# Two cross-attention layers with mixtures of experts: zero products at the beginning, undivided GpSimd operations, a new order of work

## The chip, the cores and the metric

One core of a Trainium2 chip runs the kernel. The metric is the device time of one execution in microseconds (us); the median of three runs is 582.1 us (580.37 to 582.15). "fp32" is the usual 32-bit type, "fp32r" a rounded form of it that TensorE multiplies in one pass; an fp32 product of 128x128 by 128 columns is two matmul instructions.

## The reference

The input x has 4 batches of 512 rows of 128 numbers, the context 4 batches of 154 rows. Four layers are added to x, each on the layer norm (ln) of what came before:

```python
x = x + L0_xattn(ln(x), ctx)   # 16 heads of 8 over the 154 context rows, softmax, output product
x = x + L0_ffn(ln(x))          # 8 experts, width 512, gelu, top 2 by a softmax router
x = x + L1_xattn(ln(x), ctx)   # causal self-attention, norm, cross-attention, norm, leaky relu net, norm, relu
x = x + L1_ffn(ln(x))          # 32 experts of width 64 and a shared one, silu(g) * u, 6 of 32 by a sigmoid router
```

Every token is computed by all experts, and the router's weights (zero for those not chosen) multiply the results.

## The kernel before

The batches are the unit of work: stage A (L0_xattn), B (L0_ffn), C (L1_xattn) and D (L1_ffn), each for b = 0 to 3. Stage A runs for all batches first, up to about 135 us. Then B of one batch is interleaved with C of the batch before, and D follows; D of batches 2 and 3 ends the run, alone.

**The order of work** is written out by hand. Each engine's program is a set of generators (stages), each cut into parts by `yield`. `merged` (line 76) reads a table for the engine (PLAN_PE, PLAN_DVE and so on) with a number for each part, and issues the parts in the order of these numbers. The numbers have no other effect: at run time an engine takes its parts in that order, and waits at semaphores. So a new table is a new order of the same steps. SP's table orders the loads (x, context, weights, and the rows of router weights that `spread_first` and `spread_second` write to memory and read back to all partitions), and the store.

**The beginning.** SP issues the loads of x and of the constants (early), ScalarE those of the context, of early_rows and of the mask. ScalarE then runs a small Exp on mhalf (`warm_up`, line 901), with the activation table's load before it. GpSimd clears KN, QN, KS, VT and VM. VectorE normalises x (L425 to L448, with two steps on GpSimd, L454 and L457), and clears WT, gsc and mks (`paddings`, L1189). TensorE's program begins with a wait for the constants. Then follow the products of the context with the key and value weights (L1665), the transposes of the normalised x (L1642), the query product (L1691), the transposes of keys (L1716, L1718) and of QN (L1654), and the first maxima products (L1730), 128x308, whose row maxima VectorE takes (L1302). ScalarE copies the transposes out (L892).

**Stage B.** For each chunk of 128 hidden columns: three products of halves (high and low parts in fp32r, L1647 to L1649), gelu on ScalarE (L1006), and the second product, plain fp32 (L1854) for even chunks and in halves (L1659 to L1661) for odd ones, where ScalarE makes the high half and VectorE the low one (L1359). Four chunks make an expert: VectorE multiplies by the router's row (L1398, ty), and GpSimd adds it to acc_o (L790, called from `stage_b`).

**Stage D.** For each pair of experts (17 with the shared one): six products (L1647 to L1649), silu on ScalarE (L1137), the product with u on VectorE (L1598, one input in PSUM), the product with the router's rows CB (L1604, both inputs in SBUF), and the down product. For batches 0 and 1 that is plain fp32 (L2027). For batches 2 and 3 (`THREE`) ScalarE makes the high half WB_r, GpSimd the low one h_r (`lows_d`, L790), and TensorE does three products (L1659 to L1661), for batch 3 in two halves of the columns.

**GpSimd's operations.** `in_pieces` (L786) cuts a two-input operation into instructions of 256 columns, with one semaphore step after the last. It is used for acc_o (512 columns), the low halves of D (512), the low halves of the weights (`split1`: four of 1024 and one of 256; `split3`: four of 512 and one of 128). `split2` (L823) and norm2b (L878) are cut by loops of their own. The odd down chunk of `shh` has 128 columns.

Of the kernel before, what the change touches and what calls it, by code (L numbers as in the profile page):

```python
# [32 lines left out]
P = 128  # L33
# [58 lines left out]
class Signal:  # L92
# [11 lines left out]
    def then(self):  # L104
# [7 lines left out]
    "constants": [[6, 979, 10456]],  # L112
    "load_x": [[0], [973], [2503], [4860]],
    "load_context": [[856], [4380], [7188]],
    "second_weights": [[16147, 25499, 34539, 35632, 36068, 38842]],
    "load_context1": [[13685], [18833], [30509], [36074]],
    "store": [[43977], [50106], [53327], [56038, 56075]],
    "spread_first": [[13075, 13317, 13323, 14187, 14774, 15464, 16141, 16845, 17432], [18839, 19144, 19150, 19625,
        20571, 21096, 22238, 23076, 23801], [25250, 25493, 25505, 26247, 27091, 27873, 29108, 29590, 30503], [31432,
        31674, 31828, 32987, 33839, 34533, 35626, 36953, 37319]],  # L120
    "spread_second": [[36329, 36929, 36941, 37325, 37337, 39097, 39249, 39412, 40036, 40168, 40629, 40767, 41092,
# [7 lines left out]
    "norm_a": [[570, 598], [1602, 1702], [4147, 4174], [7093, 7121]],  # L129
    "values": [[1620], [4736], [7645], [10442]],  # L130
    "key_tails": [[1803, 1861], [4278, 4560], [7858, 7919], [9331, 11489]],
    "norm_b": [[7726, 7754], [11468, 11547], [16027, 16054], [23214, 23241]],
    "stage_b": [[14690, 14838, 15464, 16158, 16845, 17432, 18020, 18542], [19625, 20571, 21096, 22395, 23076, 24397,
        24544, 24932], [26247, 27091, 27873, 29291, 29590, 30761, 31022, 31828], [34140, 34288, 34533, 35626, 37787,
        37935, 38083, 38417]],
    "split1": [[31631, 35782, 38556, 38832, 41808]],
    "split2": [[12971, 14410]],
    "split3": [[39108, 39972, 40111, 40817, 50723]],
    "lows_d": [[48235, 48748, 48908, 49301, 49440, 49692, 49898, 50038, 50350, 50585, 50939, 51077, 51242, 51569,
        51775, 52038, 52176], [52382, 52709, 52847, 53119, 53325, 53463, 53669, 53875, 54081, 54287, 54493, 54820,  # L140
        54959, 55203, 55341, 55547, 55685]],
    "stage_c": [[18957, 18985, 22264, 22291, 23532, 23559, 24255, 25665, 25692], [25537, 25564, 28559, 28587, 30630,
        30657, 31493, 32807, 32834], [32361, 32388, 35764, 36058, 37150, 37177, 37646, 39277, 39304], [39149, 39176,
        42795, 42822, 44984, 45011, 45723, 47076, 47103]],
    "norm_d": [[29160, 29187], [34120, 34671], [40799, 40955], [48373, 48400]],
}
PLAN_ACT = {
    "warm_up": [[0, 18]],
    "split0": [[2564, 2614, 3385, 3588, 3864, 3913, 4785, 6718]],
    "prepare_a": [[1033], [2663], [5153], [8263]],  # L150
    "query_stacks": [[1512, 1886, 2050, 3257], [3990, 4640, 5334, 5983], [7002, 7697, 7996, 8878], [9548, 10494, 10890,
        11666]],
    "key_stacks": [[1270, 1305, 1340, 1375, 1413, 1561, 1596, 1631], [3135, 3222, 3637, 3777, 4406, 4441, 4476, 4511],
        [6648, 6683, 6819, 6854, 7373, 7460, 7495, 7530], [8994, 9028, 9247, 9281, 10195, 10282, 10317, 10352]],
    "group": [[2110, 2224, 2274, 2339, 2388, 2460], [2712, 2833, 2886, 2996, 3080, 3173, 3435], [3336, 3487, 3539,
# [6 lines left out]
    "output": [[5104], [7938], [10786], [13437]],  # L162
    "prepare_b": [[10992, 12302, 13012], [15446, 18137, 18592], [20899, 22292, 25187], [27171, 29383, 31368]],
# [193 lines left out]
def build_program(nc, a):  # L357
# [1270 lines left out]
    def _(pe):  # L1628
# [4 lines left out]
        def claim(k):  # L1633
            if last_read[k]:
                pe.wait_ge(*last_read[k])
# [497 lines left out]
```

## Time and profile before

| | us |
|---|---|
| median of three runs | 582.1 |
| the profiled execution | 581.68 |
| its span, first to last instruction | 579.9 |
| TensorE busy | 554.4 (96%) |
| VectorE busy | 446.9 (77%) |
| ScalarE busy | 378.5 (65%) |
| GpSimd busy | 190.8 (33%) |

PE is TensorE (PEld its weight loads), DVE VectorE, ACT ScalarE, POOL GpSimd, SP the queue that issues loads. Busy time counts an instruction from start to end; matmuls overlap, so their ends run past the start of the next. In the stages, each engine's busy us is followed by its number of instructions (x...), then come the granted clock of TensorE (1.00 is full), the busy share of the DMA engines and GB/s. A group's row has the line, the engine, the operation, out<-in, the shapes and the count, then busy us and mean ns of one, then idle time before it and what ended it. A row in order of time has start, length, then the same names; equal instructions are merged (x...).

### The profile page before, as it was taken

Reading aid. Unit: us, or ns where it says so; the run is one execution under the profiler, and the core shown is the slowest. Engines: PE = TensorE matmul, PEld = TensorE weight load, DVE = VectorE, ACT = ScalarE, POOL = GpSimd, SP = SyncE. Lnnn points to the kernel's source line nnn. Section 1 sums busy time; section 2 is a strip of 40 time slices with the busy share of each in tenths; the row PEclk is TensorE's granted clock in tenths of the full one; section 3 lists DMA queues with packets and bytes.
Section 4 is the critical chain, followed back from the end, with each engine's and each line's share of the span. In section 5 each row is a group of like instructions: output and inputs, shape, how many; then the busy total and the mean of one; then the engine's idle time right before and its main releaser. Section 6 shows DMA issues by size and latency. Waiting matters only on the chain.

```text
span 579.9 us, 8752 instructions
## 1 busy us (share of the span) xinstructions
PE 554.4 (96%) x2629; PEld 389.6 (67%) x2629; DVE 446.9 (77%) x1343; ACT 378.5 (65%) x663; POOL 190.8 (33%) x265
## 2 busy tenths in 40 slices
PE   4899999999999999999999999999999999999996
PEld 3566566655777677667767677667566766776885
DVE  6898999882454566879577796978988999889774
ACT  2587677757767797757875599865664623565653
POOL 3102020011433112443133413448341011477765
PEclk9999999999999999999999999999999999999998
DMA  4401000301111111003101102441121432432440
GB/s 142 176 20 29 1 9 2 121 25 42 42 47 36 47 37 37 20 18 93 36 20 45 39 19 74 141 110 62 67 90 42 145 92 77 143 114 67 149 151 20
DMA packets 23327, 38.40 MB, mean 66 GB/s; under 512 B 3792, under 2 KB 9552, under 8 KB 22896
## 3 DMA queue, kind: packets, MB, share of 16 engines
q1 hardware_dynamic: 22848, 37.44, 20.6%
q8 instruction: 21, 0.34, 0.2%
q10 hardware_dynamic: 432, 0.40, 0.2%
q14 instruction: 26, 0.21, 0.1%
HBM read 36.45 MB, written 1.38 MB: 65 GB/s over the span
## 4 chain that ended last, share of the span: by engine, by line
PE 72%; DVE 12%; POOL 6%; ACT 4%; issue 4%; DMA 1%; POOLq 0%; DVEq 0%; ACTq 0%
PE ps L1647 9%; PE ps L1649 8%; PE ps L1648 8%; PE ps L1854 7%; PE ps L2027 4%; PE ps L1730 3%; PE ps L1659 3%; PE ps L1660 3%; PE ps L1661 3%; PE ps L1654 3%; PE ps L1750 3%; PE ps L1764 2%; PE ps L1642 2%; PE ps L1767 2%; POOL w1s L790 2%
## 5 line engine op out<-in xcount | busy, mean ns | idle before, releaser
L1647 PE MATMUL ps<-xThi,w1s 128*128 128x512 f32 x256 | 122.8, 480 | 3.0 <-DVE h L1598 1.5
L1006 ACT ACTIVATE h<-ps,early 128x512 f32<-128x512 f32 x128 | 86.2, 686 | 54.8 <-PE ps L1649 48.4
L1649 PE MATMUL ps<-xTlo,w1s 128*128 128x512 f32 x256 | 100.8, 394 | 0.0
L1648 PE MATMUL ps<-xThi,w1s 128*128 128x512 f32 x256 | 100.4, 392 | 0.0
L1137 ACT ACTIVATE s<-ps 128x512 f32<-128x512 f32 x68 | 40.7, 599 | 57.4 <-PE ps L1649 55.7
L790 POOL TENSOR_TENSOR acc_o<-acc_o,ty 128x256 f32<-128x256 f32 x64 | 52.2, 836 | 76.9 <-DVE ty L1398 76.1
L1359 DVE TENSOR_TENSOR h_r<-h,s_r 128x512 fp32r<-128x512 f32 x64 | 48.9, 766 | 26.2 <-ACT s_r L892 26.0
L1854 PE MATMUL ps<-h,w2s 128*128 128x512 f32 x128 | 66.1, 598 | 2.6 <-DVE ty L1398 2.6
L1647 PEld LDWEIGHTS ps<-xThi,w1s 128*128 128x128 f32 x256 | 48.2, 188 | 29.4 <-DVE h L1598 9.0
L790 POOL TENSOR_TENSOR h_r<-h,WB_r 128x256 fp32r<-128x256 f32 x68 | 54.3, 823 | 31.4 <-ACT WB_r L892 31.3
L1302 DVE TENSOR_REDUCE NM<-ps 128x2 f32<-128x308 f32 x128 | 56.6, 472 | 9.5 <-PE ps L1730 7.9
L1598 DVE TENSOR_TENSOR h<-s,ps 128x512 f32<-128x512 f32 x68 | 46.4, 683 | 18.4 <-PE ps L1649 15.1
L1648 PEld LDWEIGHTS ps<-xThi,w1s 128*128 128x128 f32 x256 | 48.3, 189 | 14.4 <-issue 8.7
L1649 PEld LDWEIGHTS ps<-xTlo,w1s 128*128 128x128 f32 x256 | 48.0, 188 | 11.1
L1604 DVE TENSOR_TENSOR h<-h,CB 128x512 f32<-128x512 f32 x64 | 52.7, 823 | 1.3
L1730 PE MATMUL ps<-KS,QS 128*128 128x308 f32 x128 | 41.8, 371 | 2.6 <-DVE NM L1302 1.7
L892 ACT ACTIVATE s_r<-h 128x512 fp32r<-128x512 f32 x64 | 39.8, 629 | 1.1
L1659 PE MATMUL ps<-s_r,w2h 128*128 128x512 f32 x64 | 40.5, 633 | 0.0
L1661 PE MATMUL ps<-h_r,w2h 128*128 128x512 f32 (+1 forms) x112 | 40.5, 362 | 0.0
L1398 DVE TENSOR_TENSOR ty<-ps,WB 128x512 f32<-128x512 f32 x32 | 22.0, 687 | 23.0 <-PE ps L1661 20.6
L958 ACT ACTIVATE h<-ps 128x512 f32<-128x512 f32 x54 | 31.2, 597 | 11.7 <-PE ps L1750 10.4
L1730 PEld LDWEIGHTS ps<-KS,QS 128*128 128x128 f32 x128 | 24.2, 196 | 15.2 <-DVE NM L1302 8.3
(291 smaller groups left out, 1150.9 us busy)
## 6 DMA issues: line engine op xcount, KB each, us to landing
CB<-ct_rows SPq DMA_DIRECT2D x128, 128.0 KB, 2.9
WB<-wt_rows SPq DMA_DIRECT2D x32, 256.0 KB, 3.2
w2s<-w_dram SPq DMA_DIRECT2D x2, 2048.0 KB, 9.7
raw<-gu_dram SPq DMA_DIRECT2D x4, 512.0 KB, 4.2
x_in<-x_dram SPq DMA_DIRECT2D x4, 256.0 KB, 3.2
w2s<-dn_dram SPq DMA_DIRECT2D x1, 1024.0 KB, 7.2
out_dram<-ty SPq DMA_DIRECT2D x3, 256.0 KB, 3.0
late<-late_dram SPq DMA_DIRECT2D x1, 608.5 KB, 8.6
```

The costliest lines, as they stand in the source:

```text
L790: last = nc.gpsimd.tensor_tensor(out[:, q], a[:, q], b[:, q], op)
L1006: nc.scalar.activation(h32[:, c % HR, :], bank[c % 2], ACT.Gelu, bias=b1T[:, c:c + 1]).then_inc(b_gelu.sem, 1)
L1302: V.tensor_reduce(NM[:, i, h:h + 2], src, AX.X, ALU.max, negate=True).then_inc(a_nm.sem, 1)
L1359: V.tensor_tensor(h32r[:, o, :], h32[:, o, :], hh0[:, j % 2, :].bitcast(F32), ALU.subtract).then_inc(b_lo.sem, 1)
L1604: V.tensor_tensor(h, h, CB[:, slot, :], ALU.mult).then_inc(d_h.sem, 1)
L1647: M(dst, w[0], xThi[:, x, :], start=start, stop=False)
L1648: M(dst, w[1], xThi[:, x, :], start=False, stop=False)
L1649: return M(dst, w[0], xTlo[:, x, :], start=False, stop=stop)
L1659: M(dst, whi, xhi, start=start, stop=False)
L1661: return M(dst, whi, xlo, start=False, stop=stop)
L1730: M(bank[u % 2][:, 0:2 * LK].rearrange("p (h k) -> p h k", h=2), QS[:, g, i * P:(i + 1) * P], KS[:, g, 2 * half:2 * half + 2, 0:LK], start ...
L1854: M(bank[2], w2s[:, c * P:(c + 1) * P], h32[:, c % HR, :], start=at, stop=ends).then_inc(b_y.sem, 1)
```

## The change

TensorE gets 24 products of the cleared WT with itself into bank 4, which nothing reads: twelve ahead of its other work and twelve between its steps. The first waits for WT's memset, which moves to the head of VectorE's program. The wait for the constants moves from TensorE's head into the first batch's `context_keys`, `context_values` and `inputs`. `in_pieces` goes, and `split1`, `split2`, `split3`, `lows_d`, `stage_b` and norm2b each issue one instruction of the full width. All five tables have new numbers, with the same steps in them apart from the 24 new ones.

```diff
 PLAN_SP
-    "constants": [[6, 979, 10456]],
+    "constants": [[6, 1001, 9526]],
-    "second_weights": [[16147, 25499, 34539, 35632, 36068, 38842]],
-    "load_context1": [[13685], [18833], [30509], [36074]],
+    "second_weights": [[13941, 27111, 32012, 35573, 36612, 38770]],
+    "load_context1": [[14311], [19728], [26057], [35579]],
...
 PLAN_ACT
-    "warm_up": [[0, 18]],
+    "warm_up": [[0, 2118]],
...
 PLAN_DVE
-    "paddings": [[558, 8109, 9079]],
+    "paddings": [[0, 557, 1985]],
...
 PLAN_PE
+    "idle_turns": [[75, 142, 187, 232, 277, 322, 366, 411, 456, 501, 546, 590, 776, 798, 869, 954, 976, 1203, 1226,
+        1433, 1455, 1478, 1500, 1601]],
-    "context_keys": [[832], [1613], [4765], [7798]],
-    "context_values": [[719], [4315], [7124], [9993]],
+    "context_keys": [[720], [1556], [4747], [7756]],
+    "context_values": [[824], [4364], [7107], [10148]],
...
+    NIDLE = 24
...
-        def in_pieces(n, out, a, b, op, width=256):
-
-            for c in range(0, n, width):
-                q = slice(c, min(c + width, n))
-                last = nc.gpsimd.tensor_tensor(out[:, q], a[:, q], b[:, q], op)
-            return last
...
-                in_pieces(S, h32r[:, t % HR, :], h32[:, t % HR, :], hh1[:, t % 2, :].bitcast(F32), ALU.subtract).then_inc(d_lo.sem, 1)
+                nc.gpsimd.tensor_tensor(h32r[:, t % HR, :], h32[:, t % HR, :], hh1[:, t % 2, :].bitcast(F32), ALU.subtract).then_inc(d_lo.sem, 1)
...
-                in_pieces(S, acc_o[:], acc_o[:], ty[:, e % 2, :], ALU.add).then_inc(b_acc.sem, 1)
+                nc.gpsimd.tensor_tensor(acc_o[:], acc_o[:], ty[:, e % 2, :], ALU.add).then_inc(b_acc.sem, 1)
...
+        def idle_turns():
+
+            for n in range(NIDLE):
+                yield
+                if not n:
+                    pe.wait_ge(pads.sem, 1)
+                claim(4)
+                M(bank[4][:, 0:P], WT[:, 0, 0:P], WT[:, 0, 0:P], start=True, stop=True)
+                read_by(4, pads, 1)
+
         def context_keys(b):
             yield
+            if not b:
+                pe.wait_ge(early_loaded.sem, 32)
...
-        pe.wait_ge(early_loaded.sem, 32)
-        merged(PLAN_PE, ("context_keys", map(context_keys, every)), ...
+        merged(PLAN_PE, ("idle_turns", [idle_turns()]), ("context_keys", map(context_keys, every)), ...
```

## Rows read from the trace of the kernel before

**Rows 1.** Stages of the run: busy us of PE, PEld, DVE, ACT, POOL; clock; DMA share; GB/s

```profile
6.10:22.40 16.30, 12.88 (x48) 10.18 (x48) 13.38 (x59) 5.22 (x11) 3.28 (x9) 1.00 0.67 223
22.40:566.00 543.60, 532.40 (x2531) 372.33 (x2532) 426.32 (x1269) 367.28 (x642) 175.30 (x235) 1.00 0.20 62
480.00:566.00 86.00, 84.43 (x391) 64.65 (x391) 71.15 (x151) 46.34 (x76) 51.26 (x65) 1.00 0.36 115
```

**Rows 2.** Chain of waits, 8 to 21 us: start, us, what

```profile
8.83 1.13 PE ps L1642 x4
...
10.64 2.08 PE ps L1691 x8
12.71 0.21 PE ps L1716
...
15.54 1.10 PE ps L1654 x4
...
17.31 0.88 PE ps L1730 x2
```

**Rows 3.** Groups of TensorE's instructions, 6 to 22.4 us

```profile
L1730 PE MATMUL ps<-KS,QS 128*128 128x308 f32 x8 | 3.6, 554 | 1.0 <-ACT QS L892 0.7 <-DVE NM L1302 0.3
L1665 PE MATMUL ps<-early,ctxA 128*128 128x128 f32 x12 | 3.1, 431 | 6.1 <-DMA mask<-mask_dram 6.1
```

**Rows 4.** The same, 22.4 to 60 us

```profile
L1730 PE MATMUL ps<-KS,QS 128*128 128x308 f32 x42 | 13.0, 357 | 0.7 <-DVE NM L1302 0.6
...
L1665 PE MATMUL ps<-early,ctxA 128*128 128x128 f32 x8 | 1.2, 275 | 0.0
```

**Rows 5.** VectorE in order of time, 0 to 6 us

```profile
5.55 0.91 DVE L1189 MEMSET WT<- 128x1024 f32 x1 [0.16 <-issue]
```

**Rows 6.** ScalarE in order of time, three stretches; then TensorE beside the last

```profile
0.72 0.44 ACTq L896 DMA_DIRECT2D ctxA<-ctxT_dram  x1
...
2.15 1.28 ACT L901 ACT_TABLE_LOAD   x1 [2.15 <-issue]
...
21.78 0.60 ACT L892 ACTIVATE QS<-ps 128x512 fp32r<-128x512 f32 x1 [3.16 <-PE ps L1654]
...
394.26 1.28 ACT L1137 ACT_TABLE_LOAD   x1 [3.66 <-PE ps L1661]
395.55 0.60 ACT L1137 ACTIVATE s<-ps 128x512 f32<-128x512 f32 x1
...
394.48 0.39 PE L1649 MATMUL ps<-xTlo,shs 128*128 128x512 f32 x1
```

**Rows 7.** Groups of GpSimd's instructions, the whole run

```profile
L790 POOL TENSOR_TENSOR h_r<-h,WB_r 128x256 fp32r<-128x256 f32 x68 | 54.3, 823 | 31.4 <-ACT WB_r L892 31.3
L790 POOL TENSOR_TENSOR acc_o<-acc_o,ty 128x256 f32<-128x256 f32 x64 | 52.2, 836 | 76.9 <-DVE ty L1398 76.1
...
L790 POOL TENSOR_TENSOR shh<-shd,shh 128x128 fp32r<-128x128 f32 x1 | 0.5, 463 | 0.0
```

**Rows 8.** GpSimd, then VectorE, in order of time, 546.5 to 551 us

```profile
546.63 1.44 POOL L790 TENSOR_TENSOR h_r<-h,WB_r 128x256 fp32r<-128x256 f32 x2 [0.95 <-ACT WB_r L892]
548.77 2.59 POOL L790 TENSOR_TENSOR h_r<-h,WB_r 128x256 fp32r<-128x256 f32 x3 [0.71 <-ACT WB_r L892]
...
549.49 1.28 DVE L1604 TENSOR_TENSOR h<-h,CB 128x512 f32<-128x512 f32 x1
```

**Rows 9.** Groups of VectorE's instructions, 480 to 566 us

```profile
L1604 DVE TENSOR_TENSOR h<-h,CB 128x512 f32<-128x512 f32 x35 | 30.8, 880 | 0.9
L1598 DVE TENSOR_TENSOR h<-s,ps 128x512 f32<-128x512 f32 x38 | 26.0, 685 | 13.0 <-PE ps L1649 11.8 <-ACT s L1137 0.9
```

**Rows 10.** Two stretches of the end; GpSimd in order of time

```profile
571.70:575.10 3.40, 1.93 (x14) 1.52 (x13) 0.05 (x1) 0.68 (x2) 2.79 (x4) 1.00 0.01 2
575.10:579.90 4.80, 2.04 (x9) 1.17 (x7) 0.85 (x2) 0.77 (x2) 0.00 (x0) 0.50 0.19 55
...
571.83 2.79 POOL L790 TENSOR_TENSOR h_r<-h,WB_r 128x256 fp32r<-128x256 f32 x4 [0.63 <-ACT WB_r L892]
```

More of the change, by code:

```diff
@@ L136 @@
[L136 to L144, printed above, removed]
@@ new lines @@
+    "masks": [[754, 775], [1494, 1515], [4734, 4825], [7519, 7556]],
+    "keys": [[887, 985, 1018, 1049, 1103], [1744, 2631, 2664, 2695, 3050], [4831, 5171, 5711, 6088, 6258], [7917, 8546,
+        8617, 8648, 8721]],
+    "values": [[1461, 1854, 2465, 2479, 2501, 2515], [4638, 4683, 4720, 4741, 4864, 5071], [7365, 7563, 7661, 7675,
+        8370, 8384], [10268, 10430, 10486, 10821, 11088, 11102]],
+    "queries": [[1158, 1230, 1293, 1306], [2991, 3310, 3614, 3627], [5849, 6125, 6188, 6388], [8483, 9067, 9130, 9220]
+        ],
@@ new lines @@
+    "context_keys": [[720], [1556], [4747], [7756]],
+    "context_values": [[824], [4364], [7107], [10148]],
+    "inputs": [[899, 1037], [2378, 2881], [5134, 5740], [8194, 8351]],
+    "queries": [[1378, 1688, 1944, 3066], [3982, 4795, 4911, 5921], [6824, 7619, 8000, 8836], [9516, 10473, 10861,
+        11662]],
+    "keys": [[1148, 1257], [3559, 3748], [6595, 7300], [8919, 9419]],
+    "maxima": [[1525, 1539, 1625, 1664, 1732, 1756, 1827, 1866], [1919, 1988, 2048, 2080, 2133, 2184, 2229, 2276],
[7 rows of a table added]
@@ new lines @@
+    "prepare_b": [[10641, 11519, 12824], [15687, 17325, 18503], [19336, 21013, 23741], [27123, 27562, 31110]],
+    "first": [[12729, 13169, 13459, 13620, 13688, 13850, 13918, 14214, 14282, 14509, 14732, 14801, 15028, 15096, 15320,
[8 rows of a table added]
+    "weights": [[13311], [19016], [25875], [32779]],
+    "second": [[13534, 13990, 14059, 14145, 14354, 14440, 14578, 14664, 14873, 14959, 15165, 15251, 15460, 15730,
[8 rows of a table added]
+    "stage_c": [[16103, 17503, 19260, 19380, 19633, 19719], [25964, 26040, 26224, 26310], [32364, 32733, 32868, 32954]
+        , [38731, 39465, 39738, 39893]],
@@ L820, in split2 @@
                 pool.wait_ge(w2_hi.sem, w2_hi.at(0, k + 1))
-                for c in range(8 * k, 8 * k + 8, 2):
-                    hi = w2h[:, c * P:(c + 2) * P].bitcast(F32).rearrange("p (c k) -> p c k", k=P)
-                    last = nc.gpsimd.tensor_tensor(odd_low[:, c:c + 2, :], odd[:, c:c + 2, :], hi, ALU.subtract)
-                last.then_inc(w2_lo.sem, 1)
+                o, c = slice(8 * k, 8 * k + 8), slice(1024 * k, 1024 * k + 1024)
+                nc.gpsimd.tensor_tensor(odd_low[:, o, :], odd[:, o, :], w2h[:, c].bitcast(F32).rearrange("p (c k) -> p c k", k=P),
+                                        ALU.subtract).then_inc(w2_lo.sem, 1)
         def split3():
@@ L830, in split3 @@
                 w, hi, low = down1_piece(k)
[L831 removed]
+                nc.gpsimd.tensor_tensor(low, w, hi.bitcast(F32), ALU.subtract).then_inc(dn_lo.sem, 1)
         def lows_d(b):
@@ L876, in stage_c @@
                 pool.wait_ge(c_a3.sem, c_a3.at(b, 0))
-            for i in range(0, NT, 2):
-                last = nc.gpsimd.tensor_tensor(norm2b[:, i:i + 2, :], norm2[:, i:i + 2, :], over_tiles(rows["b2f"], 2), ALU.add)
-            last.then_inc(c_n2b.sem, 1)
+            nc.gpsimd.tensor_tensor(norm2b[:], norm2[:], over_tiles(rows["b2f"]), ALU.add).then_inc(c_n2b.sem, 1)
             yield from ln_n3.gpsimd(pool, b)
@@ L1676, in context_values @@
             yield
+            if not b:
+                pe.wait_ge(early_loaded.sem, 32)
             pe.wait_ge(a_ctx_in.sem, a_ctx_in.at(b, 32))
@@ L1683, in inputs @@
             yield
+            if not b:
+                pe.wait_ge(early_loaded.sem, 32)
             pe.wait_ge(ln_a.out.sem, ln_a.out.at(b, NT))
```

233 lines of the change are left out of this document (112 added, 121 removed), and 198 rows, old and new, of tables (PLAN_ACT, PLAN_DVE, PLAN_PE, PLAN_SP).

## The prediction, made before the changed kernel ran

> **What bounds the kernel now.** I read the stages first, then the chain of waits, then single instructions. The stages show TensorE busy 532.40 of 543.60 us from 22.4 to 566 [rows 1]. Whatever is done there, at most 11.2 us of idle TensorE can be won, because the work itself does not shrink. The beginning is different: nothing on TensorE until 6.1 us [rows 3], and 12.88 of 16.30 us until 22.4 [rows 1].
>
> The beginning has a second peculiarity. The granted clock reads 1.00 there, but the durations don't. The same 128x128 fp32 product of L1665 takes 431 ns before 22.4 us and 275 ns after, and the 308-column product of L1730 takes 554 and 357 ns [rows 3, 4]. I read this as the lower level (1.2 GHz) until 22.4 us and 2.4 GHz from there, with no record of the throttle printed for the first stretch. Its last stretch has the record: 0.50 after 575.1 us [rows 10]. So 16.3 us of the kernel run at half rate. What TensorE did before the rise: one group after another from 17.3 us on. The steady stream from 10.64 (eight halves of products, then transposes until 14.7) raised nothing [rows 2, 3].
>
> **Zero products and the clock.** The wait for the constants' load leaves the head of TensorE's program for the three steps that use them, and 24 products of WT's zeros are added, twelve ahead of everything. They need WT cleared. That memset takes 0.91 us and stood at 5.55, after the first statistics; it moves to the head of VectorE's program, where nothing runs until the x load has landed [rows 5]. Other engines' first work starts at 0.72 us [rows 6], so I put WT's zeros at 1.6 us. An fp32 product is two instructions, and at the low level these start 0.213 us apart (0.21 for one in the chain, 2.08 for eight with the pipeline's end of 0.38 [rows 2]). Twelve products are 24 x 0.213 = 5.1 us: 1.6 to 6.7 at worst. The real work begins when the early load has landed at 6.1 [rows 3], so up to 0.6 us of delay. What hides it: the next step on the chain begins at 8.83 and waits for VectorE's xn, not for these products [rows 2]. Then TensorE has been busy without a gap from 1.6 to about 8 us, longer than the whole stretch from 17.3 to 22.4 that ended with the rise. I take the clock to be up by 8 us.
>
> The other twelve go between the steps of 7 to 16 us. At the high level each costs 0.21 us, 2.6 us in all, in a stretch where TensorE idles 16.30 - 12.88 = 3.4 us and will idle 6 us more once its work is halved. They cost nothing if warm.
>
> What the path gains, step by step, at half of the low-level issue time. Transposes at 8.83: four instructions, 4 x 0.107 = 0.43, and a shorter end, 0.5 together. Query products at 10.64: eight, 0.9, with the end 1.0. Transposes of the keys, of which the chain passes through four from 12.71 on: 0.4. Those of QN at 15.54: four, 0.45. Sum of the four: the first maxima product comes 2.35 us earlier than 17.31 [rows 2]. From there to 22.4 the chain has 4.1 us of TensorE (its first piece is 0.88 for two L1730 [rows 2]; seven pieces like it, of L1730, L1665 and L1654, make the sum). Halved that is 2.0, but VectorE's maxima are next: its share in 6.1 to 22.4 is 13.38 of 16.30 us [rows 1]. I take 0.9, near the middle of 0 and 2.0. **Sum: -3.2 us**, bounds -4.4 and 0. A shift at the head of a stretch that is 97% busy is carried to the end; no load fixed in time stands in it, since the DMA share there is 0.20 [rows 1].
>
> **ScalarE's warm-up** (the Exp that waits for mhalf) moves from the head to behind the first query stack. The table load before it starts at 2.15 and takes 1.28 us. Would the first copy at 9.98 now pay it? At 394.26 a load starts while the product its activation waits for is still running, so it stands ahead of that wait [rows 6]. It should again run in the first microseconds. The small Exp lands in an idle of 3.16 us [rows 6]. Cost: 0, and 1.28 us if the load sits behind the wait, which is the far bound. The Trainium skill (ScalarE: Activation LUTs, What ACT_TABLE_LOAD costs) adds a drain to the load, 2.66 us in all; by it the far bound would be 2.7 us. The trace disagrees: the activation behind the load of 394.26 starts at 395.55, with 0.01 us between them [rows 6].
>
> **GpSimd undivided.** Pieces of 256 columns take 836 ns (acc_o, x64) and 823 ns (h_r, x68); an undisturbed pair takes 1.44 us. One of 128 columns takes 463 ns [rows 7, 8]. From 0.463 and 0.72 for twice the columns, 512 columns come to 0.72 + 2 x 0.257 = 1.24 us, an estimate: 0.2 us less than the pair. The pairs are 32 of acc_o, 34 of h_r, four of norm2b and four of the down weights, and the splits of 1024 columns are four pieces each. Seventy-four pairs save 15 us of an engine that is 51.26 of 86 us busy at its worst [rows 1], and its idle time hides almost all of it. It is on the path only where the pieces end a chain: in the tail, the last two lows are four pieces in 2.79 us behind which TensorE waits [rows 10]. Two undivided ones are 2.5. **Sum: -0.3 us.**
>
> Against it stands a collision. VectorE's L1604 reads two SBUF tiles and takes 880 ns in 480 to 566, while L1598, with one input from PSUM, keeps 685 [rows 9]. In a close view, L1604 begins at 549.49 with GpSimd's second piece and takes 1.28 us: it gets the port when the piece has ended, and in 548.77 to 551.36 the third piece is longer for it [rows 8]. A piece blocks for at most 0.72 us. Undivided, it blocks for 1.24, but GpSimd is no longer interrupted in the middle. The excess is 35 x (0.880 - 0.693) = 6.6 us in this stage. If the wait grows by 1.24/0.72, another 4.7 us, VectorE is at 71.15 + 4.7 = 76 of 86 us, under TensorE's 84.43 [rows 1]. I take +0.4 us for what gets through, bounds -1 (GpSimd's own stretched pieces) and +4.7. The Trainium skill (GPSIMD Engine Reference, section 1) says that GpSimd's way to SBUF is shared with VectorE and meets its instructions with two SBUF inputs; the trace agrees, 880 ns against 685.
>
> **Order of work.** All five programs are reordered, SP's loads among them. In front of the waiting instruction now stand others: load_context1 of batch 2 moves from behind spread_first of batch 2 to its second entry, so the WB rows of that batch queue behind a wait for the context product of batch 1. Those rows have a whole expert's time to land. The w2 load comes earlier, second_weights stands nearer the head, and none is on the chain of the beginning. How well a new order fits can't be read from these rows; the idle of 11.2 us bounds what it may win, and half of that is a fair bound for a loss. I take 0, with 1.5 us to either side, since both orders keep the same steps and dependences.
>
> **Total.** 581.68 (the profiled execution; span 579.9) - 3.2 - 0.3 + 0.4 = **578.6 us**. The median before is 582.1, 0.4 above that execution, so this is 0.6% faster than the median. About 0.3%, 1.75 us, is what can be told from no change: under 580.35 is faster, over 583.85 is slower.
>
> **Rivals.**
> (1) *The zeros do not raise the clock.* The trace has no product of zeros. Then the twelve later ones cost 0.43 each in the chain: 0.2 before the query products, 0.4 before the second keys, 1.0 and 0.4 around the first maxima, +2.0 us, and the whole is 581.7 + 2.0 + 0.1 = 583.9, slower. It decides if durations of 430 ns last past 8 us. For it: only real data did it before. Against: the level rose on activity, and nothing shows it to be of values. Chance 0.08.
> (2) *The clock rises and falls again* between 8 and 15 us. The records show a fall at 575.1 after a stretch with TensorE busy 1.93 of 3.40 us [rows 10]. After the change 8 to 15 holds about 1.7 us of transposes, 1.3 of products and 1.9 of zero products in 7 us, no denser than that. Against it: no fall is on record between 22.4 and 575.1, through many stretches of small steps. A fall loses the gain of one part and delays the rest by the dearer zeros: -1.2 instead of -3.2, 580.6. Chance 0.17.
> (3) *Undivided operations hold VectorE.* The full +4.7 us or its like in the other stages gets through where VectorE, not TensorE, ends the wait: 581.7 - 3.5 + 4.0 = 582.2. For it: VectorE is 83% busy at the end; against: L1598, half of its work there, is untouched. Chance 0.13.
> (4) *The new order loses* 2 us: 580.6. Chance 0.10. The forecast has 0.52.
>
> **How the numbers follow.** The forecast's own range is 576.5 to 580.6. With rivals 2, 3 and 4 the range becomes 576.2 to 582.6; outside lie rival 1 and the far end of each. Faster: 0.50 of the forecast, half of 2 and 4 (0.13), none of 3: 0.63. Slower: 0.08 and 0.03 of rival 3. Same: 0.26.
>
> **What would show it.** Durations of L1665 at 6 to 8 us between 431 and 275, and L1691 at 10 us at 275; the first L1730 product near 15 us; all later stages about 3 us earlier. GpSimd's acc_o group x32 at 1.25 to 1.4 us. L1604 at 480 to 566 no more than 1.0 us. It is wrong if the first maxima come at 17 us, or if TensorE's idle between 22.4 and 566 grows by over 2 us, which would be the collisions or the order.

## The result, and the profile after

The kernel after takes **573.28 us** (median of four runs, 573.03 to 574.52) beside 581.69 us for the kernel before on the same chip: ratio 0.9868, interval 0.9851 to 0.9885, 8.4 us by the medians or 7.7 us by the ratio. The forecast was 578.6 with a range down to 576.2: the direction was right, the gain was more than twice the 3.5 us forecast, and the time lies 2.9 us below the range. The profiled execution of the kernel after is the slowest of its four (574.52 us; span 572.7).

From the page of the kernel after: busy time by engine, the chain by engine, and six groups (columns as before: busy us, mean ns, then the idle time ahead of them and its releaser).

```profile
PE 556.3 (97%) x2677; PEld 393.5 (69%) x2677; DVE 447.4 (78%) x1343; ACT 376.1 (66%) x663; POOL 170.1 (30%) x173
...
PE 86%; DVE 6%; ACT 3%; issue 2%; POOL 1%; DMA 1%; POOLq 0%; SPq 0%; ACTq 0%; DVEq 0%
...
L862 POOL TENSOR_TENSOR acc_o<-acc_o,ty 128x512 f32<-128x512 f32 x32 | 43.6, 1361 | 85.1 <-DVE ty L1391 80.0
...
L1863 PE MATMUL ps<-h,w2s 128*128 128x512 f32 x128 | 65.8, 596 | 0.3 <-DVE ty L1391 0.3
...
L1352 DVE TENSOR_TENSOR h_r<-h,s_r 128x512 fp32r<-128x512 f32 x64 | 48.1, 752 | 14.7 <-ACT s_r L885 14.5
...
L833 POOL TENSOR_TENSOR h_r<-h,WB_r 128x512 fp32r<-128x512 f32 x34 | 47.6, 1409 | 28.4 <-ACT WB_r L885 28.1
...
L1597 DVE TENSOR_TENSOR h<-h,CB 128x512 f32<-128x512 f32 x64 | 52.9, 827 | 1.2
...
L1739 PE MATMUL ps<-KS,QS 128*128 128x308 f32 x128 | 42.6, 376 | 1.6 <-DVE NM L1295 1.4
```

Seven lines of most steps are gone, so L1604 of before is L1597 now. The pairs of 836 and 823 ns [rows 7] have become single operations of 1361 and 1409 ns. The chain that ended last is TensorE's own for 86%.

The stages of the kernel after (columns as in [rows 1]):

```profile
6.10:22.40 16.30, 13.75 (x92) 11.56 (x92) 14.68 (x64) 6.38 (x14) 3.34 (x9) 1.00 0.64 224
22.40:135.00 112.60, 108.31 (x625) 68.79 (x629) 95.51 (x328) 81.53 (x156) 13.35 (x27) 1.00 0.08 27
135.00:390.00 255.00, 252.93 (x1138) 179.43 (x1137) 181.82 (x540) 192.04 (x331) 75.79 (x68) 1.00 0.16 51
390.00:480.00 90.00, 89.89 (x401) 63.08 (x400) 81.17 (x262) 47.60 (x83) 22.95 (x21) 1.00 0.25 86
480.00:560.00 80.00, 78.99 (x371) 60.12 (x370) 67.59 (x135) 43.25 (x73) 44.55 (x33) 1.00 0.38 121
560.00:572.70 12.70, 8.31 (x44) 6.42 (x42) 4.28 (x7) 4.00 (x8) 5.46 (x5) 0.79 0.08 23
```

From 390 to 480 us TensorE is idle for 0.11 of 90 us. Between 22.4 and 560 the idle is 7.5 us, where the kernel before had 11.2 to 566 [rows 1]. That is 3.7 us of the 7.2 that the span lost; 2.3 us come from ahead of the first exp, and the other 1.2 us lie behind these stretches (13.9 us of the run before, 12.7 now). The borders of 566 and 560 us don't cut the work at the same step, so the three parts are a rough division.

TensorE of the kernel after in order of time, 1.9 to 16 us:

```profile
1.97 5.49 PE L1668 MATMUL ps<-WT 128*128 128x128 f32 x24 [1.97 <-DVE WT L1182]
7.26 0.75 PE L1658 MATMUL ps<-early,ctxA 128*128 128x128 f32 x4
...
8.96 0.60 PE L1635 MATMUL ps<-early,xn 128*128 128x128 f32 x4
...
10.25 1.16 PE L1700 MATMUL ps<-early,xT 128*128 128x128 f32 x8 [0.24 <-ACT xT L885]
...
15.13 0.56 PE L1739 MATMUL ps<-KS,QS 128*128 128x308 f32 x2
```

Twelve zero products (24 instructions) run from 1.97 us. The trace's record of full rate begins at 7.55 us, where it began at 22.15 before. The eight query products take 1.16 us and not 2.08 [rows 2], and the first maxima product stands at 15.13 and not 17.31: 2.18 us earlier, where my working had 2.35. The part of the forecast about the beginning came out as told.

The marks of later steps (the start of the same step of ScalarE in both profiles) do not fit it. Against the kernel before, the first gelu is 0.9 us ahead (139 us), the last gelu 3.5 us (389 us), the nineteenth silu 7.3 us (452 us), the end 7.1 us. Of the 2.3 us at the first exp, 1.4 are lost again by 139 us (1.2 of them in one wait for a load, last section). Then 6.4 us are won between 139 and 452 us, where the forecast had nothing.

### The profile page after: what moved, and what is told of

The parts are those of the page before. It is cut to its first block, busy times and chain, and to the rows that moved or that the text cites. A ratio compares the mean times of both kernels' runs of the same rounds, so it can differ in the third digit from the quotient of the medians.

```text
span 572.7 us, 8759 instructions
## 1 busy us (share of the span) xinstructions
PE 556.3 (97%) x2677; PEld 393.5 (69%) x2677; DVE 447.4 (78%) x1343; ACT 376.1 (66%) x663; POOL 170.1 (30%) x173
## 3 DMA queue, kind: packets, MB, share of 16 engines
q1 hardware_dynamic: 22848, 37.44, 20.1%
HBM read 36.45 MB, written 1.38 MB: 66 GB/s over the span
## 4 chain that ended last, share of the span: by engine, by line
PE 86%; DVE 6%; ACT 3%; issue 2%; POOL 1%; DMA 1%; POOLq 0%; SPq 0%; ACTq 0%; DVEq 0%
PE ps L1640 11%; PE ps L1642 10%; PE ps L1641 10%; PE ps L1863 8%; PE ps L2036 5%; PE ps L1652 4%; PE ps L1739 4%; PE ps L1653 3%; PE ps L1654 3%; PE ps L1759 3%; PE ps L1635 3%; PE ps L1647 2%; PE ps L1773 2%; PE ps L1776 2%; PE ps L1940 2%
## 5 line engine op out<-in xcount | busy, mean ns | idle before, releaser
L862 POOL TENSOR_TENSOR acc_o<-acc_o,ty 128x512 f32<-128x512 f32 x32 | 43.6, 1361 | 85.1 <-DVE ty L1391 80.0
L1352 DVE TENSOR_TENSOR h_r<-h,s_r 128x512 fp32r<-128x512 f32 x64 | 48.1, 752 | 14.7 <-ACT s_r L885 14.5
L833 POOL TENSOR_TENSOR h_r<-h,WB_r 128x512 fp32r<-128x512 f32 x34 | 47.6, 1409 | 28.4 <-ACT WB_r L885 28.1
L1642 PEld LDWEIGHTS ps<-xTlo,w1s 128*128 128x128 f32 x256 | 48.0, 188 | 11.2
L1597 DVE TENSOR_TENSOR h<-h,CB 128x512 f32<-128x512 f32 x64 | 52.9, 827 | 1.2
L1739 PEld LDWEIGHTS ps<-KS,QS 128*128 128x128 f32 x128 | 22.9, 188 | 20.1 <-DVE NM L1295 14.1
```

The source lines that it names most:

```text
L833: nc.gpsimd.tensor_tensor(h32r[:, t % HR, :], h32[:, t % HR, :], hh1[:, t % 2, :].bitcast(F32), ALU.subtract).then_inc(d_lo.sem, 1)
L1352: V.tensor_tensor(h32r[:, o, :], h32[:, o, :], hh0[:, j % 2, :].bitcast(F32), ALU.subtract).then_inc(b_lo.sem, 1)
L1597: V.tensor_tensor(h, h, CB[:, slot, :], ALU.mult).then_inc(d_h.sem, 1)
L1642: return M(dst, w[0], xTlo[:, x, :], start=False, stop=stop)
L1739: M(bank[u % 2][:, 0:2 * LK].rearrange("p (h k) -> p h k", h=2), QS[:, g, i * P:(i + 1) * P], KS[:, g, 2 * half:2 * half + 2, 0:LK], start ...
```

## Experiments: the three parts, one by one and together

**The parts by themselves.** The kernel before with the zero products alone (table, 24 products, WT cleared first, the wait for the constants moved as in the change):

```diff
+    NIDLE = 24
...
+        merged(PLAN_PE, ("idle_turns", [idle_turns()]), ("context_keys", ...
```

> The kernel before with the 24 zero products alone (and WT's memset at VectorE's head); old order, pieces of 256. Theory Z (the clock carries most of the 8.4 us): at or under 576. Theory S (the clock is worth what the stages of the beginning show, 2 to 4 us): 578 to 580, with the first maxima near 15.5 to 16.5 us. Theory O or G (order or undivided operations carry it, and the lead of the beginning is lost again by 60 us, as in the changed kernel's marks): 580.5 to 581.7, although the clock is up by 8 us.

Measured: 579.39 us beside 581.75, ratio 0.9955 (0.9940 to 0.9971). The lead at the first exp is 2.14 us and stays within 0.05 us of that up to 541 us. A shift at the head is carried to the end, as the forecast had it.

The kernel before with only GpSimd's operations undivided, old order:

```diff
-                in_pieces(S, acc_o[:], acc_o[:], ty[:, e % 2, :], ALU.add).then_inc(b_acc.sem, 1)
+                nc.gpsimd.tensor_tensor(acc_o[:], acc_o[:], ty[:, e % 2, :], ALU.add).then_inc(b_acc.sem, 1)
```

(and the same for `split1`, `split2`, `split3`, `lows_d`, norm2b)

> The kernel before with undivided GpSimd operations alone; old order, no zero products. Theory G (GpSimd's shorter operations carry most of the gain): 575 to 577. Theory O: within 1 us of 581.7. My prediction's term: +0.1 us (gain 0.3 at the end, loss 0.4 by collisions).

Measured: 584.32 us, ratio 1.0035 (1.0024 to 1.0046). Undivided operations lose 2 us in the old order.

The kernel after with its operations back in pieces of 256 columns:

> The changed kernel with GpSimd's operations cut to 256 columns again; new order, zero products. Theory G: 579 or more. Theory O: 573 to 574.5, the order does not mind. If order and undivided operations only work together: above 576, while e2 shows no gain.

Measured: 578.29 us, ratio 0.9929 (0.9906 to 0.9951). In the new order the same edit is worth a gain, 3.5 us by the ratios.

The kernel after without the zero products:

> The changed kernel without the 24 zero products; new order, undivided operations. Theory Z: 579 or more. Theory S: 575.5 to 577. Theory O or G with a lead that is lost by 60 us anyway: 573 to 574.5, the rise of the clock late (over 15 us).

Measured: 576.20 us, ratio 0.9895 (0.9873 to 0.9917).

**The missing corners.** The old order with zeros and undivided operations, and the new order with neither:

> The kernel before with the zero products and the undivided operations, in the old order. If the two parts add in the old order, as they did one by one (-2.36 us for the zeros, +2.57 us for the undivided operations, beside 581.75 us), the time is 581.95 us. If the later start of the zeros' clock lets the undivided operations do their harm earlier or later, it differs from that by over 1 us. Against the kernel after (573.3 us) it is the same work in the old order: the order is then worth some 8.7 us of the time when the operations are undivided.

Measured: 582.31 us, ratio 1.0006 (0.9995 to 1.0018).

> The new order alone: operations in pieces, no zero products. If zeros are worth the same in the new order with pieces (578.3 us with them) as elsewhere (2.4 to 2.9 us), the time is 580.7 to 581.2 us, so that the new order alone gains 0.5 to 1 us over 581.75 us, inside the plus or minus 1.5 us I gave it. If the order is worth 8 us by itself whatever the operations, it would be 573 to 575 us.

Measured: 579.96 us, ratio 0.9971 (0.9957 to 0.9984).

The eight corners, as ratios to the kernel before:

| | old order | new order | the order is worth |
|---|---|---|---|
| pieces, no zeros | 1 | 0.9971 | -1.7 us |
| pieces, zeros | 0.9955 | 0.9929 | -1.5 us |
| undivided, no zeros | 1.0035 | 0.9895 | -8.1 us |
| undivided, zeros | 1.0006 | 0.9868 | -8.0 us |

Read down a column, the zeros are worth -2.6, -1.7, -2.4 and -1.6 us: a part by itself. The undivided operations are worth +2.0 and +3.0 us in the old order, -4.4 and -3.5 in the new one. They and the order are one change: 6.4 to 6.5 us are there only when both are (8.1 - 1.7 without zeros, 8.0 - 1.5 with them; the intervals of the four ratios, added in squares, make that 6.4 ± 1.6 and 6.5 ± 2.0). My sum had them as two terms.

## Experiments: which operations

Four kernels put one kind of operation back into pieces in the new order, or make one kind undivided in the old one.

> The kernel after, with only the 32 additions to acc_o in pieces of 256 columns (the 68 low halves of the last stages stay undivided). The profile of the kernel after with all in pieces lost 0.7 us until 390 us, some 1.2 us by 430 us and the rest after 547 us. If the loss belongs to the stage whose operations are cut, cutting acc_o alone costs 0.7 to 1 us here: 574.0 to 574.5 us. If the acc_o additions drive the whole difference by the order's fit, it is near 578 us.

Measured: 574.98 us, ratio 0.9879 (0.9859 to 0.9899).

> The kernel after, with only the low halves of h (34 operations in the last stages) in pieces of 256 columns, two 0.73 us operations each in place of one of 1.24 to 1.4 us. If the loss belongs to the last stages (some 4 of the 5.0 us, by the marks), the time is 576.5 to 577.5 us, with the last down products waiting for GpSimd. If it is the additions to acc_o that make it, it is near 573.5 us.

Measured: 576.27 us, ratio 0.9904 (0.9889 to 0.9920). Its marks lie within 0.15 us of the kernel after up to 391 us, and within 0.5 us up to 534; the loss comes behind that, 2.6 us at the last but one silu. The groups of GpSimd, VectorE and TensorE from 540 to 575 us, of the kernel after and then of this one:

```profile
L833 POOL TENSOR_TENSOR h_r<-h,WB_r 128x512 fp32r<-128x512 f32 x14 | 19.8, 1427 | 8.5 <-ACT WB_r L885 8.2
L1597 DVE TENSOR_TENSOR h<-h,CB 128x512 f32<-128x512 f32 x12 | 14.2, 1181 | 0.4
L1652 PE MATMUL ps<-WB_r,w2h 128*128 128x256 f32 x29 | 8.9, 308 | 1.7 <-POOL h_r L833 1.6
```

```profile
L793 POOL TENSOR_TENSOR h_r<-h,WB_r 128x256 fp32r<-128x256 f32 x28 | 23.4, 862 | 7.5 <-ACT WB_r L892 7.5
L1604 DVE TENSOR_TENSOR h<-h,CB 128x512 f32<-128x512 f32 x12 | 10.5, 874 | 0.4
L1659 PE MATMUL ps<-WB_r,w2h 128*128 128x256 f32 x29 | 8.9, 307 | 3.4 <-POOL h_r L793 3.4
```

A pair takes 1.72 us, an undivided operation 1.43, and the down product's wait for it grows from 1.7 to 3.4 us. The tables say why the new order is hurt. Their entries count about hundredths of a microsecond (the last low half stands at 55747 and began at 565.92 us). The distance from a low half's entry (`lows_d`) to its down product's, over the 34 of batches 2 and 3, has its median at 2.44 us in the old tables, the least 1.48; in the new ones 1.89, the least 1.36, nine under 1.45. The shortest distance from one low half's entry to the next, six times over, is 1.38 us in the old tables and 1.26 in the new: the one is near an undisturbed pair (1.43 to 1.44 us before), the other near an undisturbed single operation (1.25 to 1.29 after). The new order leaves room for one undivided operation and no more.

> The kernel before, with only the 32 additions to acc_o undivided. If these hold VectorE's low halves back in the expert stages (with all undivided, the loss was 2.3 us by 323 us of 2.6 us, and TensorE's idle time before the down products of these stages rose from 0.03 to 2.6 us), the time is 583 to 584 us. If it is another of the undivided operations (the weights' low halves lie in the same stretch), it stays at 581.8 us.

Measured: 582.36 us, ratio 1.0005 (0.9996 to 1.0015).

> The kernel before, with only the 34 low halves of h in the last stages undivided. In the kernel with all undivided the last stages lost only 0.3 us and the end gained a little: 581.5 to 582.1 us. In the new order the same edit gained 2.1 us of ratio (undivided against pieces); if that is the operations' own worth, and not the order's, it is 579.5 to 580 us here.

Measured: 581.25 us, ratio 0.9994 (0.9985 to 1.0003). Neither interval shows a loss. The profile of e13 does lose 1.1 us between the first gelu and the last, 0.5 us of it where TensorE waits for VectorE's low half before a down product at 304.60 us, and most of it is back by the nineteenth silu. What is left:

```diff
-                in_pieces(w, dst[:, 1, c:c + w], raw1[:, k % 2, 0:w], dst[:, 0, c:c + w].bitcast(F32),
-                          ALU.subtract).then_inc(gu_lo.sem, 1)
+                nc.gpsimd.tensor_tensor(dst[:, 1, c:c + w], raw1[:, k % 2, 0:w], dst[:, 0, c:c + w].bitcast(F32),
+                                        ALU.subtract).then_inc(gu_lo.sem, 1)
```

> The kernel before, with only the low halves of the weights (1024 columns undivided: 2.4 us) and the norm2b additions undivided. If these make the loss by themselves, the ratio is that of all undivided, 1.0035 (583.5 to 584.3 us), with TensorE waiting before the down products of the expert stages right behind them. If the loss comes only where they meet undivided additions to acc_o, it stays near 1.001 (582 to 582.7 us).

Measured: 582.91 us, ratio 1.0017 (1.0006 to 1.0029): of the three kinds the only one whose interval lies above 1. By the ratios it is 1.0 us, half or less of the 2.0 to 3.0 that all undivided operations cost in this order. One place shows how. The weights' low half w2s_r in the kernel before (four pieces), then in this one: GpSimd, VectorE, TensorE, in order of time.

```profile
150.98 3.34 POOL L823 TENSOR_TENSOR w2s_r<-w2s,w2h 128x256 fp32r<-128x256 f32 x4 [11.89 <-ACT w2h L892]
...
151.46 0.81 DVE L1359 TENSOR_TENSOR h_r<-h,s_r 128x512 fp32r<-128x512 f32 x1 [2.29 <-ACT s_r L892]
```

```profile
152.21 2.38 POOL L822 TENSOR_TENSOR w2s_r<-w2s,w2h 128x1024 fp32r<-128x1024 f32 x1 [12.35 <-ACT w2h L889]
...
152.69 2.45 DVE L1356 TENSOR_TENSOR h_r<-h,s_r 128x512 fp32r<-128x512 f32 x1 [2.29 <-ACT s_r L889]
...
155.19 0.50 PE L1656 MATMUL ps<-s_r,w2h 128*128 128x512 f32 x1 [0.93 <-DVE h_r L1356]
```

VectorE's low half takes 0.68 us undisturbed. Started 0.48 us into GpSimd's operation, it takes 2.45: it gets nothing until that has ended at 154.59, and needs its own time then. Beside four pieces it took 0.81. TensorE stands for 0.93 us before the down product, and the marks behind (the ninth gelu against the seventeenth) have lost 1.19 us. A second such place at 370 us costs 0.8 us (VectorE 2.53 us, TensorE's wait 1.16). The groups of TensorE from 135 to 390 us, in the kernel before and then in this one:

```profile
L1854 PE MATMUL ps<-h,w2s 128*128 128x512 f32 x124 | 63.9, 597 | 1.9 <-DVE ty L1398 1.9
...
L1659 PE MATMUL ps<-s_r,w2h 128*128 128x512 f32 x62 | 38.9, 627 | 0.0
```

```profile
L1851 PE MATMUL ps<-h,w2s 128*128 128x512 f32 x124 | 63.8, 596 | 1.0 <-DVE ty L1395 1.0
...
L1656 PE MATMUL ps<-s_r,w2h 128*128 128x512 f32 x62 | 38.7, 624 | 2.1 <-DVE h_r L1356 2.1
```

Both effects are there: the wait before the second products falls by 0.9 us, and a new one of 2.1 us stands before the down products.

The three kinds together have 0.0016 of the ratio, all at once 0.0035 without zeros and 0.0051 with them. The marks suggest why the parts do not add. From the first gelu to the last, e17 loses 1.6 us, e13 1.1 and e2 2.8, which is their sum. Between the first and the nineteenth silu e17, e13 and e2 each win back 1.0 to 1.2 us: a slack that seems to be there once, however much was lost ahead of it. That rests on one profile of each and is not shown. (The 1.7 us by which the profile of e17 ends behind that of the kernel before are no measure: 1.2 of them stand already at the first gelu, full rate having begun at 26.74 us and not 22.15.)

The same operation in the kernel after, GpSimd and then VectorE:

```profile
153.65 2.71 POOL L818 TENSOR_TENSOR w2s_r<-w2s,w2h 128x1024 fp32r<-128x1024 f32 x1 [19.07 <-ACT w2h L885]
...
153.43 0.68 DVE L1352 TENSOR_TENSOR h_r<-h,s_r 128x512 fp32r<-128x512 f32 x1
154.03 2.35 DVE L444 TENSOR_TENSOR ln_b_t<-ln_b_t,ln_b_y 128x4 f32<-128x4 f32 x1
156.29 0.68 DVE L1352 TENSOR_TENSOR h_r<-h,s_r 128x512 fp32r<-128x512 f32 x1
```

VectorE is blocked here too, on a sum of four columns that takes 2.35 us; TensorE waits for nothing at this place. One low half is done just ahead of the block (it began first, and GpSimd's operation is 0.3 us longer for it), the next just behind, in time. At 391.73 us two such operations of GpSimd (4.74 us together) lie beside VectorE's operations with an input in PSUM and its statistics of one input, none of which is longer for it:

```profile
391.31 0.69 DVE L1488 TENSOR_TENSOR a<-ps,norm2b 128x512 f32<-128x512 f32 x1 [0.89 <-PE ps L1980]
392.05 0.69 DVE L1591 TENSOR_TENSOR h<-s,ps 128x512 f32<-128x512 f32 x1
392.66 0.68 DVE L1394 TENSOR_TENSOR X<-ps,X 128x512 f32<-128x512 f32 x1
393.98 0.69 DVE L1591 TENSOR_TENSOR h<-s,ps 128x512 f32<-128x512 f32 x1 [0.64 <-PE ps L1642]
394.58 0.87 DVE L427 BATCH_NORM_STATS2 ln_n_st<-a 128x6 f32<-128x128 f32 x4
```

There are six operations of 1024 columns in each kernel. In the old order (e17) two of them hold a low half that TensorE waits for, 2.1 us in all. In the new order four hold nothing, one the sum above, and one, at 352.01 us, a low half (1.82 us and not 0.68), for which TensorE does not wait:

```profile
352.01 2.38 POOL L810 TENSOR_TENSOR w1s<-raw,w1s 128x1024 fp32r<-128x1024 f32 x1
...
353.12 1.82 DVE L1352 TENSOR_TENSOR h_r<-h,s_r 128x512 fp32r<-128x512 f32 x1
```

So the new order has the long operations beside work that they can't block, or that nobody waits for at that time. That accounts for some 2 us of the 8. The Trainium skill (SBUF — State Buffer, Terms) says that the port pair of VectorE and GpSimd is taken for a full instruction and the loser waits for all of it; the four places agree, 2.45, 2.53, 2.35 and 1.82 us.

> The kernel after, with only the low halves of the weights and the norm2b additions in pieces of 256 columns. All in pieces cost 0.0061 of the ratio (3.5 us), acc_o alone 0.0011, the low halves of h alone 0.0036; if the parts add, 0.0014 is left: ratio 0.9882, some 574 to 574.8 us. If the parts hide each other, it is the ratio of the kernel after, 0.9868.

Measured: 575.05 us, ratio 0.9887 (0.9866 to 0.9908). In the new order the three kinds in pieces cost 0.0011, 0.0036 and 0.0019, together 0.0066; all at once 0.0061. They add, within their intervals. Only the middle one, the low halves of h, has an interval clear of the kernel after's.

## Experiments: the order, the zeros, the end

**Parts of the order.** The old tables (zeros and undivided operations in all three), with the new entries for one third of the steps on all engines:

> The kernel before with zero products and undivided operations (its own measurement: 582.31 us, ratio 1.0006), and of the new tables only the entries of the first attention stages (0 to 140 us) on all engines. Theory A, the order gains by stage where its work lies: with the same operations the new order is 0.3 us ahead of the old one at 139 us, so 582.0 us. Theory B, the new order pays only as a whole because its parts fit each other: the mixture loses, 583 us or more.

Measured: 592.97 us, ratio 1.0198 (1.0182 to 1.0215).

> The same kernel with old order, and of the new tables only the entries of the first expert stages (the gelu chunks, their high and low halves, the additions to acc_o, the weights' loads; 130 to 390 us) on all engines. Theory A: between 139 and 390 us the new order takes 4.8 us more lead over the old one with the same operations, and most of TensorE's idle time that goes stands before the down products of these stages: 577.5 to 579 us. Theory B: 582 us or more.

Measured: 604.67 us, ratio 1.0395 (1.0380 to 1.0410).

> The same kernel with old order, and of the new tables only the entries of the last stages (silu chunks, their halves, router, down products, output; 380 us to the end) on all engines. Theory A: TensorE's idle time from 390 to 560 us falls from 3.83 to 1.12 us between the old and the new order with the same operations: 579.3 to 580 us. Theory B: 582 us or more.

Measured: 588.56 us, ratio 1.0119 (1.0104 to 1.0133).

Against 1.0006 with all tables old, they lose 11, 23 and 7 us. Every mixture loses, as theory B had it. But a mixture has seams that neither order has, and its loss doesn't price the third that was put in. Groups of TensorE's instructions with long new waits, of e9 (0 to 45 us) and then of e10 (whole run):

```profile
L1593 PE MATMUL ps<-KS,QS 128*128 128x308 f32 x27 | 10.8, 442 | 8.0 <-DVE NM L1149 7.8
```

```profile
L1494 PE MATMUL ps<-xThi,w1s 128*128 128x512 f32 x256 | 123.8, 484 | 7.4 <-ACT h L853 4.9 <-DVE h L1445 1.3 <-ACT s L984 0.4
...
L1784 PE MATMUL ps<-early,PN 128*128 128x128 f32 x40 | 7.1, 274 | 3.8 <-ACT PT L739 3.8
```

In e9 the maxima are late mainly for one reason. The second batch's x stands at 995 in the new table of the loads, the weights behind it at 979 in the old one, so in the mixture the weights go first; each whole table has x first (973 before 979, 995 before 1001). The load of x is issued at 13.32 us and not at 9.40 (e5, second fence), and VectorE, whose maxima stand behind that x in its queue, waits 7.06 us:

```profile
13.32 0.41 SPq L555 DMA_DIRECT2D x_in<-x_dram  x1
...
21.25 0.87 DVE L281 BATCH_NORM_STATS2 ln_a_st<-x_in 128x6 f32<-128x128 f32 x4 [7.06 <-DMA x_in<-x_dram]
```

```profile
9.40 0.38 SPq L700 DMA_DIRECT2D x_in<-x_dram  x1
```

At the first exp e9 is 7.3 us behind e5, at the first gelu 10.9, and nothing is lost after. So e9 shows what one pair of loads in the wrong order costs, and says little of the attention stages' order. In e10 the loss grows over the whole stretch from 180 to 390 us, at TensorE's waits for ScalarE's gelus and for the small steps of the attention (ACT PT above). The clock is part of it: TensorE was busy 1.22 of the 4.10 us before 317.1 us and 2.31 of the 4.10 before 375.1, and half rate followed, 6.8 and 3.4 us long. In e9 it was at half rate from 20.1 to 30.3 us, behind its wait of 6.83 us. How much of the losses the clock makes is not separated.

**The transfers.** SyncE's table was also exchanged by itself:

> The kernel after, with the table of SyncE's transfers of the kernel before. If the transfers' order has no part in the gain: 573 to 574 us. If weights or combine weights come late at places that the new order needs them earlier, over 575 us, with TensorE or VectorE waiting for DMA.

Measured: 575.42 us, ratio 0.9884 (0.9871 to 0.9898). Its profile shows one loss of its own, 0.6 us between 209 and 224 us, where TensorE waits for VectorE's ty; the rest of its distance comes from the clock at the beginning (below). TensorE's waits for loads do not grow. The two intervals overlap, so the order of the transfers is at most a small part.

**Half of the zeros.**

> The kernel after, with the first 12 of the 24 zero products (they end near 5 us, the first real product stands at 7.26 us). If the last twelve are needed to keep the clock from going the old way, it is up at 15 us or later and the time is 575 to 576.2 us, as without any. If twelve raise it as well, 573.3 us.

Measured: 574.97 us, ratio 0.9873 (0.9853 to 0.9892), not to be told from the kernel after. Full rate begins at 7.62 us in its profile, so the first twelve products are enough to raise the clock. In that profile it is lost again from 17.86 to 24.69 us, the first exp comes at 24.94 us (24.88 in e4, without zeros), and the span is that of e4, 572.6 beside 572.7 us. Whether the other twelve help to keep the clock up stays open: it falls in this stretch in five of the twelve profiles with all 24, and stays up in seven.

**The end.** The last two low halves of h go to VectorE:

```diff
-            for n in range(ND):
+            for n in range(ND - 2 * (b == NB - 1)):
...
+        def last_lows():
+            for n in range(ND - 2, ND):
+                yield
+                t = (NB - 1) * ND + n
+                if n == ND - 2:
+                    dve.wait_ge(d_lo.sem, d_lo.at(NB - 1 - THREE, n))
+                dve.wait_ge(d_hi.sem, d_hi.at(NB - 1 - THREE, n + 1))
+                V.tensor_tensor(h32r[:, t % HR, :], h32[:, t % HR, :], hh1[:, t % 2, :].bitcast(F32), ALU.subtract).then_inc(d_lo.sem, 1)
```

> The kernel after, with the last two of the 34 low halves of h on VectorE, which stands idle for 5.0 us there, in place of GpSimd, which does them one after the other (2.50 us for two). If GpSimd's queue at the end is what TensorE waits for (1.39 us before the last but one chunk), the last chunks' products start some 0.6 us earlier and the last follows without a gap: 1.0 to 1.5 us faster than the kernel after, 571.8 to 572.3 us. If the clock or the last high half on ScalarE sets the end, it stays at 573.3 us.

Measured: **571.91 us**, ratio 0.9833 (0.9819 to 0.9847), faster than both kernels. The last chunks in the kernel after (GpSimd, TensorE), then here (VectorE, TensorE):

```profile
564.70 2.50 POOL L833 TENSOR_TENSOR h_r<-h,WB_r 128x512 fp32r<-128x512 f32 x2 [1.10 <-ACT WB_r L885]
...
566.01 0.38 PE L1652 MATMUL ps<-WB_r,w2h 128*128 128x256 f32 x1 [1.39 <-POOL h_r L833]
...
567.25 0.53 PE L1652 MATMUL ps<-WB_r,w2h 128*128 128x256 f32 x1 [0.25 <-POOL h_r L833]
```

```profile
564.13 1.36 DVE L1615 TENSOR_TENSOR h_r<-h,WB_r 128x512 fp32r<-128x512 f32 x2 [0.32 <-ACT WB_r L886]
...
564.88 0.39 PE L1662 MATMUL ps<-WB_r,w2h 128*128 128x256 f32 x1 [0.84 <-DVE h_r L1615]
```

Two operations take 1.36 us in place of 2.50, and one wait goes. Between the last silu and the end this profile has 8.71 us, that of the kernel after 10.49. Not all of these 1.8 us belong to the edit: the kernel after fell to half rate at 567.34 us (0.53 us for the product that took 0.38), and e4, e15, e16 and e18, with the same operations in its end, did so later, at 570.8 us or after, and have 9.80 to 9.82 us there. Against these the edit wins 1.1 us, and the clock made the other 0.7. By the medians e12 is 1.4 us faster than the kernel after, by the ratios 2.0.

## Why the prediction was wrong

**"Zero products and the clock: -3.2 us."** The mechanism was right, with every sign that was named: full rate from 7.55 us, L1700 at half its old time, the first maxima at 15.13. The size is 1.6 to 2.6 us. Of the term of 0.9 us between the first maxima and 22.4 us little came: the lead grows from 2.18 us at the first maxima to 2.34 at the first exp in the kernel after, and from 1.59 to 2.14 in e1. VectorE, 14.68 of 16.30 us busy in that stretch, is likely the bound there.

**Rival 2, the clock rises and falls again,** was given 0.17 and "no fall is on record". It happens, and not only with zeros: in nine of the twenty profiled executions full rate ended between 17.9 and 20.6 us and came back between 23.1 and 30.3. In eight of them TensorE had not been idle for as much as 0.9 us at a time in the 4 us before; only that of e9 follows a long wait. The stretches 17 to 20 and 20 to 24 us of e7 (e8, with the same instructions up to there, has 1.00 in both):

```profile
17.00:20.00 3.00, 2.50 (x10) 1.45 (x10) 2.88 (x9) 0.60 (x1) 1.90 (x6) 0.94 0.96 387
20.00:24.00 4.00, 3.61 (x15) 3.08 (x15) 2.74 (x13) 1.29 (x3) 0.00 (x0) 0.61 0.48 175
```

It cost e7 1.3 us against the kernel after, by the marks on both sides of it. It is likely part of the spread between executions of one kernel: each has its mean granted clock on record, and e7's two slowest (575.47 and 576.08 us) have the lowest, 0.993, its fastest (574.29 and 574.31) 0.998 and 1.000; in e5 seven executions at 0.997 took 582.2 to 582.6 us, four at 0.999 or 1.000 took 581.2 to 581.5. No two profiles of one kernel show where in the run that is.

**"GpSimd undivided: -0.3" and "+0.4 for what gets through".** The net of +0.1 was measured as +2.0 to +3.0 in the order for which I had worked it out. Rival 3 had the mechanism, but the wrong operations: I costed the block at 1.24 us on L1604, for 512 columns. L1604 from 480 to 560 us went from 880 (to 566 us, [rows 9]) to 917 ns. In the last stretch, from 540 us, it is held indeed (1181 ns, beside 874 with pieces in e8), but no wait of TensorE's groups there is for it. What does hurt by itself are the splits of 1024 columns, which the text names as "four pieces each" and never prices. They block for 2.38 us, and what they meet is L1356 (before: L1359), VectorE's other operation with two inputs in SBUF, behind which a down product stands. They are 1.0 of the 2.0 to 3.0 us; the rest is there only with several kinds undivided together, and its cause is not shown.

**"Order of work: 0, with 1.5 us to either side."** This is the step that failed, together with its being added to the term above as if the two were independent. It is off by little for the order alone in pieces (-1.7 and -1.5 us). With undivided operations the order is worth -8.1 and -8.0 us. The reasoning had two faults. "The idle of 11.2 us bounds what it may win" is true of the sum of all parts, and 7.7 us lie inside it; I let the centre be 0 and did not ask what the order had been fitted to. The tables' own due times, with a low half's down product 1.36 us behind it and the next low half 1.26, name the duration for which they were made: an undisturbed pair of 1.44 us does not fit in that, an undisturbed single operation of 1.25 to 1.29 does. And "half of that is a fair bound for a loss" was too small by far: e10 loses 23 us with the same steps and dependences. Rival 4 priced a losing order at 2 us for the same reason.

For the new order in pieces the sum would have been near (e3: 578.29 us beside 578.6), with the zeros worth 2.4 us there and the order 1.5 to 1.7. What it missed is what undivided operations and the new order do together.

The ScalarE warm-up came out as costed: the table load runs at 2.25 us and the first copy at 9.60 does not wait.

What stays open: which of the new positions hold the 8 us. The marks say where it is won: the kernel after gains 5.4 us on e5 (old order, the rest the same) between the first gelu and the last, 2.9 more by the nineteenth silu, and nothing after. Two of the 5.4 are the waits behind the long operations. The mixtures don't decide the rest, and no run has the new table of one engine alone, SyncE's apart.

## What to carry to other kernels

When a change alters both the duration of operations and the order of work, the two are one term: run or price the order with the durations it was made for, and look in the planner's due times for which durations these are. An operation with two SBUF inputs on GpSimd blocks such operations of VectorE for its whole length, so its price is set by the longest one and by what lies beside it, not by the mean: lay it beside operations that read PSUM. Before two orders are mixed, look for pairs of steps whose due times lie close: each table here had a load of x 0.06 us ahead of the weights, the mixture had it behind them, and lost 7 us there. At the end of a kernel, look for an engine that has run out of work; two operations moved to it gave 1.1 us of the end here. And before a difference between two profiles is read as the edit's, compare where the clock fell in each.

## What the runs showed of the hardware

- A GpSimd operation of 1024 columns in 2.38 us held a VectorE operation of 4 columns for 2.35 us; VectorE's operations with one input in PSUM kept 0.68 to 0.69 us beside two of them.
- Products of zeros raise TensorE's clock as products of data do: full rate from 5.0 to 7.8 us in all profiles with them, from 14.5 to 26.7 us in all without. It can be lost again with TensorE mostly busy (above).
- SyncE's issue of the second batch's mask took 1.84 us in the kernel after and in e8, 1.72 in e12, 1.65 in e18, 1.38 in e7 and 1.34 in e16, and 0.43 in all others. TensorE waited 1.16 us for it in the kernel after:

```profile
46.69 1.84 SPq L694 DMA_DIRECT2D mask<-mask_dram  x1
...
50.71 0.71 PE L1658 MATMUL ps<-early,ctxA 128*128 128x128 f32 x4 [1.16 <-DMA mask<-mask_dram]
```

  In the new order it is there in every profile where the issue began before 48.0 us, and gone at 48.03 (e3) and later; in the old order issues at 45.40 (e1), 46.44 (e5) and 47.55 us took 0.43. The cause stays open.
